# Joining the halves of the narrow last chunk in the local feed-forward turns

## What is computed

```python
DIM = 256; HID = int(DIM * 4 * 2 / 3)      # 682
h = shift_token(x)                         # second half of the features one position later
h = (h - h.mean(-1)) / sqrt(h.var(-1) + 1e-05) * lg + lb
h = h @ w1 + b1                            # w1: 256 x 1364
a, g = split(h, 2, axis=-1)                # 682 each
h = a * gelu(g)
x = x + h @ w2 + b2                        # w2: 682 x 256
```

## Time and profile before

| | |
|---|---|
| median of 3 runs | 2656.38 us (2656.29 to 2656.98) |
| span of the profiled execution | 2656.6 us |
| layer 0 of the feed-forward turns, from the first hidden chunk | 2090.4 to 2235.5 us |
| layer 1, from the first memset to the end | 2493.3 to 2656.6 us |
| PE busy over the span | 2298.0 us (87%) |
| DVE, ACT, POOL busy | 1419.3, 1042.2, 696.8 us |
| mean granted TensorE clock | 0.928 |

### The profile page before, as it was taken

One profiled execution on the slowest core, in us unless ns is written; L12 is line 12 of the kernel. 1 busy time (PEld: TensorE's weight loads), 2 busy tenths in 40 slices (PEclk: granted clock), 3 DMA queues, 4 the chain that ended last, 5 costly groups with the idle time before them and its releaser, 6 DMA issues. The chain is left out here.

```text
span 2656.6 us, 38842 instructions
## 1 busy us (share of the span) xinstructions
PE 2298.0 (87%) x12968; PEld 1651.9 (62%) x12968; DVE 1419.3 (53%) x4229; ACT 1042.2 (39%) x2653; POOL 696.8 (26%) x669
## 2 busy tenths in 40 slices
PE   7994499988869969995698899698999898999898
PEld 5773377765547648873387666464566675466676
DVE  3565022256658857665133666454776443677454
ACT  2443111135516610063143366343666332666432
POOL 1012311110014424412544100563433101433110
PEclk9997699979959979996799899799999999999899
DMA  9113211075000010030253211300000000000000
GB/s 232 39 72 157 85 42 51 16 164 42 1 7 1 1 42 1 19 132 28 91 172 109 94 25 33 153 1 32 1 2 1 1 1 1 1 1 1 21 24 20
DMA packets 112242, 127.38 MB, mean 48 GB/s; under 512 B 46515, under 2 KB 100021, under 8 KB 110256
## 3 DMA queue, kind: packets, MB, share of 16 engines
q1 hardware_dynamic: 103312, 103.91, 14.7%
q0 software_dynamic: 8736, 20.99, 2.2%
HBM read 79.93 MB, written 47.90 MB: 48 GB/s over the span
## 5 line engine op out<-in xcount | busy, mean ns | idle before, releaser
L461 PE MATMUL bank<-weights,work 128*128 128x256 f32 (+5 forms) x1768 | 463.1, 396 | 17.1 <-DVE weights L2542 8.1
L461 PE MATMUL bank<-work,weights 128*128 128x256 f32 (+3 forms) x1680 | 409.7, 404 | 18.1 <-DVE work L4844 10.8
L461 PEld LDWEIGHTS bank<-weights,work 128*128 128x128 f32 (+2 forms) x1768 | 314.9, 191 | 113.3 <-issue 66.1
L461 PEld LDWEIGHTS bank<-work,weights 128*128 128x128 f32 (+1 forms) x1680 | 300.0, 189 | 99.4 <-DVE work L4844 14.3
L845 POOL TENSOR_TENSOR work<-work,minus_half 128x2 f32<-128x2 f32 x96 | 69.3, 722 | 849.0 <-DVE work L838 849.0
L461 PE MATMUL bank<-weights,x_feat 128*128 128x512 f32 (+2 forms) x576 | 214.6, 507 | 15.7 <-ACT weights L4420 10.0
L870 ACT COPY x_feat<-bank 128x512 f32<-128x512 f32 x80 | 46.6, 584 | 299.2 <-PE bank L862 298.8
L461 PEld LDWEIGHTS bank<-weights,x_feat 128*128 128x128 f32 x576 | 107.8, 199 | 74.9 <-issue 49.1
L4444 ACT ACTIVATE work<-work 128x128 f32<-128x128 f32 (+1 forms) x256 | 137.0, 543 | 1.6 <-DVE work L4531 1.6
L461 PE MATMUL bank<-x_feat,weights 128*128 128x256 f32 (+3 forms) x400 | 117.9, 472 | 19.9 <-PEq L247 15.2
L1775 DVE TENSOR_TENSOR work<-bank,work 128x384 f32<-128x384 f32 (+1 forms) x64 | 31.4, 491 | 189.7 <-ACT work L1693 189.7
(11 more groups left out here) (465 smaller groups left out, 4686.7 us busy)
## 6 DMA issues: line engine op xcount, KB each, us to landing
weights<-in_weights SPq DMA_DIRECT2D x1, 12296.0 KB
weights<-in_weights SPq DMA_DIRECT2D x1, 9360.0 KB
weights<-in_weights SPq DMA_DIRECT2D x1, 8488.0 KB
work<-rows_in SPq DMA_DIRECT2D x62, 129.0 KB
rows_in<-ident SPq DMA_DIRECT2D x2, 3968.0 KB, 44.0
weights<-rows_back SPq DMA_DIRECT2D x8, 768.0 KB, 4.9
work<-rows_in SPq DMA_DIRECT2D x8, 645.0 KB, 4.2
rows_in<-ident SPq DMA_DIRECT2D x2, 2560.0 KB, 34.1
```

Source lines behind the costliest of these rows:

```text
L461: ins = nc.tensor.matmul(out, lhsT, rhs, start=(i == 0), stop=(i == len(pairs) - 1))
```

## The change

The two narrow halves of chunk 5 are first copied side by side into a new tile `w_last` of 128 columns (POOL, two copies at the start of each turn). `hidden` of chunk 5 is then one sum of two matmuls with the full 128 columns, into the same partitions and columns of the bank as before. The last matmul of each group in `output` takes all 128 rows; the upper 64 rows of `hid` for chunk 5 are set to zero once per turn by DVE, and `w2` is zero there. Chunk 5 waits for the two copies.

```diff
-    x_in = A(2, 2, D)
+    x_in, w_last = A(2, 2, D), A(KT, P)
...
             nc.gpsimd.memset(eps, LN_EPS).then_inc(S.pool_step, 1)
+            for c in range(2):
+                at = (c * HT + HT - 1) * P
+                nc.gpsimd.tensor_copy(w_last[:, :, c * PART:(c + 1) * PART], w1[:, :, at:at + PART]).then_inc(S.last_copied, 1)
...
                     pe.wait_ge(S.hid_stored, n - RING + 1)
+                if n == HT - 1:
+                    pe.wait_ge(S.last_copied, 2)
...
                 else:
-                    for c in range(2):
-                        at = (c * HT + f) * P
-                        ins = mm(nc, bank[c * PART:(c + 1) * PART, 0:L],
-                                 [(w1[:, k, at:at + PART], xn[:, b % 2, k, :]) for k in range(KT)])
+                    ins = mm(nc, bank[:, 0:L],
+                             [(w_last[:, k, :], xn[:, b % 2, k, :]) for k in range(KT)])
...
                     ins = mm(nc, K.bank[Y][:, i * D:(i + 1) * D],
-                             [(hid[:, b % 2, f, i * P:(i + 1) * P], w2[:, f, :]) for f in range(HT - 1)] +
-                             [(hid[0:PART, b % 2, HT - 1, i * P:(i + 1) * P], w2[0:PART, HT - 1, :])])
+                             [(hid[:, b % 2, f, i * P:(i + 1) * P], w2[:, f, :]) for f in range(HT)])
...
+            nc.vector.memset(hid[PART:P, :, HT - 1, :], 0.0)
             for t in range(STEPS):
```

More of the change, by code:

```diff
@@ L67, in signals_of_even_turns @@
     S.y_added = S.gelu_done = sem("y_added_or_gelu_done")
-    S.table_done = S.slots_loaded_2 = sem("table_done_or_slots_loaded_2")
+    S.table_done = S.slots_loaded_2 = S.last_copied = sem("table_done_or_slots_loaded_2_or_last_copied")
     S.slot_done = S.k_stored = sem("slot_done_or_k_stored")
```

## The result

The changed kernel takes 2636.35 us, the median of 4 runs (2633.89 to 2639.95); the kernel before, on the same chip, 2656.34 (4 runs, 2655.04 to 2656.98). The ratio is 0.9931, 95% interval 0.9917 to 0.9945. The forecast was 2641.5 with a range of 2637.5 to 2647: faster, as forecast, and by 5 us more than the sum. The profiled execution of after spans 2632.9 us, 3.4 less than the median, that of before 2656.6.

What follows compares the result with a forecast made beforehand. PE bounds both feed-forward turns, in layer 1 also the loop through DVE and POOL. Gains of 8.1 us in layer 0 and 6.8 in layer 1, together 14.9, take 2656.38 to 2641.5 us, range 2637.5 to 2647.

Steps and rivals of the forecast that it cites:

- narrow chunk: Hidden chunk 5 on PE: joining its halves removes the change of shape at entry and exit, saving 0.35 us each.
- output group: End of each output group on PE: a full last matmul saves 0.39 us, 0.20 at entry and 0.19 at exit.
- Layer 1: Feed-forward layer 1: 0.59 us a batch on the DVE and POOL loop, 0.27 from the race; 6.8 us in all.
- The race: Layer 1, shared DVE/POOL ports: first L4838 turns from 0.11 us behind POOL's addition to 0.08 ahead, gaining 0.27 a batch.
- The copies: Two POOL copies before the bias additions: 0.6 us later start in layer 0, ends 0.3 and 1.1; nothing in layer 1.
- The rest of layer 1: Layer 1 outside the steady batches: 0.05 first narrow chunk, 0.93 last full batch, 1.5 last two outputs and chunk 5.
- Layer 0: Feed-forward layer 0: 2.6 us from narrow chunks plus 6.05 from output groups, less 0.6 for copies: 8.1 us.
- the turns move against it, and a third more or less of such stretches is 2.5 us: Turns between the layers: some 15 us at half clock rate; variation of 2.5 us used to widen the range.
- Rival 1: Layer 1: DVE still comes second to POOL, so no 0.27 a batch; 13.5 us gained, 2642.9 us; chance 0.24.
- rivals 3 and 4: 3: unseen loop work takes all layer 1 gain, 2648.3 us, chance 0.09; 4: pause belongs to place, 2656 us, 0.06.
- Rival 2: Layer 1: both L4838 pass before POOL's first addition, some 1.2 us more a batch, 2636.9 us; chance 0.08.
- Rival 5: Layer 1: longer PE waits drop the granted clock to 1.2 GHz each batch, slower, 2666 us for example; chance 0.03.

Runs made afterwards that it cites:

- e1: Kernel before with only the joined chunk 5 and its two copies, output product as before with 64 rows and no memset: 2647.02 us, ratio 0.9973.
- e4: Kernel before with the second output group's six matmuls backwards, so the two 64-row matmuls stand side by side: 2643.93 us, ratio 0.9958.
- e2: Kernel before with only the output half: memset and full 128-row last matmul, chunk 5 in two narrow halves without copies: 2644.19 us, ratio 0.9957.
- e8: Changed kernel with POOL's two additions for a later batch made to wait until DVE has normalised: 2629.61 us, ratio 0.9902.
- e9: Changed kernel with one unused DVE memset of 256 columns ahead of each normalisation in layer 1: 2639.04 us, ratio 0.9939.
- e6: Kernel before with only the additions (copies, their wait, memset), both matmuls keeping the old operands: 2654.49 us, ratio 0.9995.
- e5: Kernel before, unedited, timed and traced again as a control: 2655.26 us, ratio 1.0001.
- e3: Changed kernel again, unedited, against the kernel before: 2635.65 us, ratio 0.9930.
- e7: Changed kernel with three unused one-column DVE memsets ahead of each normalisation in layer 1: 2637.30 us, ratio 0.9923.
- e10: Changed kernel with three POOL memsets delaying the start of the layer 0 turn: 2633.29 us, ratio 0.9925.
- e11: Kernel before with three POOL memsets delaying the start of the layer 0 turn: 2652.75 us, ratio 0.9997.
- e12: Kernel before with POOL's two additions for a later batch made to wait until DVE has normalised: 2646.15 us, ratio 0.9970.

## Why the prediction was right, and what it missed

**The shape.** 0.35 us for a narrow chunk was forecast, 0.36 measured (e1); 0.39 for an output group, 0.39 (e4) and 0.79 for two (e2). A period of layer 0 was to shorten by 1.13 and did by 1.14. The Trainium skill (TensorEngine Tiling, Key Properties) says that a change of tiling mode drains the engine; e4 agrees, with 0.39 us for a change and back. The advice of the same page to tile a stationary side of up to 64 columns (Performance Considerations) gives nothing here: the joined chunk takes four steps of 0.216, as the paired halves did, and the whole 0.36 is the change of mode that the tiling asked for.

**Layer 1.** Forecast 0.59 + 0.27 a batch, measured 0.87. That the narrow chunk gives nothing there (e1: 18.50) and that the output gives all (e2: 17.64) was forecast. The 0.59 alone is nowhere seen without the turned order; that e4, with 0.20 on the loop and the turned order, gains 0.46 fits both terms. The race itself went as worked out: DVE 0.08 ahead; POOL's first addition stretched by 0.25, beginning in effect 0.15 before the end of L4840; then the second of the L4840 held, 1.49. A period without POOL shows how much it still holds back: 17.63 against 16.40 (e8).

The Trainium skill (SBUF — State Buffer, the section on two separate sides) has it that whichever of DVE and GpSimd starts first holds the ports that they share. After agrees in its outcome. e9 differs on the face of the trace: POOL's row starts 0.19 us before DVE's multiplication and yet POOL waits for it. Either the start in the row is not the moment at which the ports are taken, or the memset ahead held them; the run does not tell these apart.

**The copies.** Forecast 0.6 in layer 0, measured 0.47; none in layer 1, and e6 as a whole is not told from before.

**The rest of layer 1.** The last full batch was to give 0.93 and gives 0.93 (15.81 to 14.88), the last one 0.97 (11.80 to 10.83). Ahead of the first residual it is 1.65 us instead of some 0.6 (0.05 and an output's 0.59): there the first 24 passes took 6.93 us, 8.50 in before, at another granted clock. This is most of what 7.89 is above 6.8.

**Layer 0** gave 6.4 instead of 8.1 in the two traces shown, and 8.0 against e5, whose turn is 158.61 and after 150.65, at 0.96 and 0.95. The turn of before shown here was the one with the better clock (0.97).

**What was mis-sized.** The step is "the turns move against it, and a third more or less of such stretches is 2.5 us", taken as plus or minus. The two feed-forward turns together came out at 14.3 to 15.7 of the forecast 14.9. What the medians have beyond it, some 4 to 6 of 20.0 us, should then lie in turns without a change; that it does is read from single traces. In the traces it is the local attention, and there it has one sign: in the six traces of kernels with the whole change (after, e3, e7 to e10) that turn takes 251.4 to 252.4 us, in before, e5 and e11 257.1, 255.7 and 254.8. The kernels with a part of it or with the additions alone lie between: 252.9 (e1), 254.8 (e2), 254.1 (e4), 254.1 (e6), 253.1 (e12). That the clock makes this difference is shown by the windows. Why it stays up is not shown: e10 speaks against the start time as the whole cause, and how closely PE's work stands in and around the turn ahead was only argued. Since e6, which runs the old shapes, has a turn 0.7 us shorter than e2 with half of the new ones, one trace for each kernel can't settle it.

The mixture turns are another matter. They take one of two lengths, 211.1 or 208.7 us and 271.6 or 269.9, in traces of either code: e6 and e11, with the old shapes, have both short, e2 and e8, with new ones, both long. So the 4.1 us that they give in the two traces shown do not go with the shapes. Where one code was traced twice (before and e5, after and e3) the lengths were the same both times; whether the program as a whole or the single execution picks the length is not shown. The 4.1 us are about what the spans differ by (23.7) beyond the medians (20.0). The Trainium skill (TensorE: Matmul & The Clock Gate, Part 1) says that the same kernel has different numbers of matmuls at the lower rate in different runs. The two traces of before agree with it: layer 0 takes 157.03 us at a clock of 0.97 in one and 158.61 at 0.96 in the other. The attention and the mixture turns together, 8.8 us, are 0.3% of the span.

**The rivals.** Rival 1 (the race stays, 2642.9) did not occur, nor did rivals 3 and 4. Rival 2's 2636.9 is almost the measured time, but its mechanism is not there: only one of the two multiplications went through, and the period of layer 1 is 17.63, not 16.7. From the median alone it would have looked right. Rival 5 did not occur: with waits of 1.0 us the clock of layer 1 is 0.96, as before, and what lowers it lies at the start of the turn; from 2500 to 2600 us it is 1.00.

## What to carry to other kernels

Where PE is the bound, look for stationary operands of two shapes in one stream: each change and back cost 0.35 to 0.39 us here, nearly two full passes. Padding with zeros, joining narrow pieces, or only grouping equal shapes side by side (e4, with no added work) took it away here. Where PE waits for a loop through DVE and POOL, first look at which POOL work can move behind DVE's (e8): it gave 7 to 8 us by two waits, and made the rest of the change count in full. And compare turn by turn: the part of a difference that lies in unchanged turns needs a control kernel before it is called a gain.

## What was not expected of the hardware

- Two mixture turns with unchanged code each take one of two lengths, 2.4 us apart in one (granted clock 0.83 or 0.84) and 1.7 in the other (0.92 or 0.93), in fourteen traces. Kernels that differ only elsewhere differ in which; what picks it is not shown.
- Where a DVE memset of 256 columns starts with a POOL addition, the DVE multiplication behind it was not held, though its row starts 0.19 us after POOL's; POOL took 1.67 us, as if its work began 0.15 us before the end of that multiplication (e9).
- Three one-column memsets ahead of a DVE multiplication moved its row by only 0.02 us, and the row starts before theirs (e7).
- fp32 copies on POOL of 128 elements per partition take 0.27 us each, much nearer the quarter of an addition (0.3) than what the prediction took from the slowest operation near it in size (0.55).
